# Second attention, its queries and its output projection in one stage; first attention's query products moved to its head; shorter expert chain

## The reference

```python
x = x + _L0_xattn_ref(_layernorm(x), ctx_1024, ctx_1024, mask, Wq, bq, Wk, bk, Wv, bv)   # first attention
x = x + _L0_attn_ref(_layernorm(x), ...)      # time mixing with a scan, channel mixing
x = x + _L0_ffn_ref(_layernorm(x), ...)       # 8 experts, the best 2
x = x + _L1_xattn_ref(_layernorm(x), ctx_1024, wq, wk, wv, wo, ln_gamma, ln_beta)        # second attention
x = x + _L1_attn_ref(_layernorm(x), ...)      # state-space scan
x = x + _L1_ffn_ref(_layernorm(x), ...)       # 8 experts, all added
```

```python
def bit_linear(x, w):
    xn = _rms_norm(x)
    xq = _ste(xn, _act_quant(xn))
    wq = _ste(w, _weight_quant(w))
    return jnp.einsum('bni,oi->bno', xq, wq)
q = bit_linear(x, wq); k = bit_linear(y, wk); v = bit_linear(y, wv)     # y: the context
out = softmax(q k / 4) v
out = layernorm(out) * ln_gamma + ln_beta
return bit_linear(out, wo)
```

## Time and profile before

| | |
|---|---|
| median of 3 runs | 1953.05 us (1948.78 to 1953.59) |
| profiled execution | 1950.69 us, span 1948.9 us |
| busy share of the span | PE 71%, DVE 69%, ACT 48%, POOL 39% |
| mean granted clock of TensorE | 0.826 of full speed |
| 38 to 206 us | first attention's tile loop |
| 682 to 758 | query stage and filling of the second attention |
| 758 to 1005 | second attention's loop over 64 batches |
| 1005 to 1058 | output projection |
| 1791 to 1949 | experts after the last scan |

### The profile page before, as it was taken

One profiled execution on the slowest core, in us unless ns is written; L12 is line 12 of the kernel. 1 busy time (PEld: TensorE's weight loads), 2 busy tenths in 40 slices (PEclk: granted clock), 3 DMA queues, 4 the chain that ended last, 5 costly groups with the idle time before them and its releaser, 6 DMA issues. The chain is left out here.

```text
span 1948.9 us, 33347 instructions
## 1 busy us (share of the span) xinstructions
PE 1383.8 (71%) x12585; PEld 772.4 (40%) x12585; DVE 1347.2 (69%) x2388; ACT 938.3 (48%) x1745; POOL 761.9 (39%) x808
## 2 busy tenths in 40 slices
PE   5889536988389514888842973445499788789998
PEld 4444223656254202555531421001145344345666
DVE  4548799961747683777769535998998899796110
ACT  2546333433134232555542434333398689676454
POOL 2325100000523123433410002664687788678433
PEclk9779777999669856999985985556599899899999
DMA  6557200000525235666621346798565465442000
GB/s 238 210 190 282 103 0 1 1 1 1 216 88 187 89 76 111 93 96 97 93 39 45 104 113 166 178 227 197 143 152 127 101 154 138 97 106 68 1 11 12
DMA packets 152100, 211.84 MB, mean 109 GB/s; under 512 B 107039, under 2 KB 112095, under 8 KB 138880
## 3 DMA queue, kind: packets, MB, share of 16 engines
q1 hardware_dynamic: 151940, 209.70, 41.5%
HBM read 154.85 MB, written 31.75 MB: 96 GB/s over the span
## 5 line engine op out<-in xcount | busy, mean ns | idle before, releaser
L2641 POOL TENSOR_TENSOR mf_st<-mf_st,mf_c_rep 128x1024 f32<-128x1024 f32 x128 | 300.9, 2351 | 339.0 <-DVE mf_st L2715 338.9
L2715 DVE TENSOR_TENSOR_SCAN mf_st<-mf_dA,mf_u_ps 128x512 f32<-128x512 f32 x256 | 310.3, 1212 | 0.0
L2543 PE MATMUL mf_y_ps<-mf_st,c_consts 128*32 128x512 f32 x512 | 155.9, 799 | 174.0 <-POOL mf_st L2641 127.1
L2826 ACT ACTIVATE mf_dA<-c_dt,c_neg_a 128x496 f32<-128x496 f32 x256 | 167.1, 701 | 108.6 <-DVE mf_st L2715 108.1
L2585 PE MATMUL mf_eh<-mf_parts,mf_w 128*128 128x512 f16 x768 | 197.4, 396 | 18.7 <-POOL mf_parts L2664 11.1
L2605 PE MATMUL mf_ey<-mf_w,mf_hid 128*128 128x256 f16 x1536 | 192.2, 276 | 0.0
L2709 DVE TENSOR_TENSOR mf_u_ps<-mf_st,mf_b_ps 128x512 f32<-128x512 f32 x256 | 177.7, 695 | 18.6 <-DMA mf_st<-xs 6.8
L2668 POOL TENSOR_TENSOR mf_hid<-mf_g,mf_hid 128x512 f16<-128x512 f32 x128 | 148.7, 1162 | 98.7 <-ACT mf_g L2843 98.6
L2605 PEld LDWEIGHTS mf_ey<-mf_w,mf_hid 128*128 128x128 f16 x1536 | 152.1, 99 | 49.3 <-issue 5.5
L2840 ACT ACTIVATE mf_hid<-mf_eh,c_vecs 128x512 f16<-128x512 f32 x128 | 88.0, 688 | 112.8 <-PE mf_eh L2585 112.3
L1978 ACT ACTIVATE t_p<-t_s_ps,t_mx 128x257 f32<-128x257 f32 x256 | 107.0, 474 | 46.8 <-DVE t_mx L2002 46.8
(11 more groups left out here) (485 smaller groups left out, 2834.3 us busy)
## 6 DMA issues: line engine op xcount, KB each, us to landing
mf_st<-xs SPq DMA_DIRECT2D x64, 1024.0 KB, 7.1
a_ctx_t<-in_ctx_t SPq DMA_DIRECT2D x16, 1024.0 KB, 7.2
a_ctx_n<-in_ctx_n SPq DMA_DIRECT2D x16, 1024.0 KB, 7.1
cqs<-a_whole_rows SPq DMA_DIRECT2D x16, 512.0 KB, 4.6
c_cq<-cqs SPq DMA_DIRECT2D x16, 512.0 KB, 13.4
mo_raw<-in_l_w SPq DMA_DIRECT2D x16, 512.0 KB, 3.7
ws<-mo_split SPq DMA_DIRECT2D x32, 256.0 KB, 2.3
mf_w<-ws SPq DMA_DIRECT2D x32, 256.0 KB, 8.6
```

The lines of the kernel that those rows point to most:

```text
L2543: m = e.matmul(y_ps[T * j:T * j + T, :], c.pick[:, gg, :], st[u % RING][:, j, :], start=(gg == 0), stop=(gg == 3))
L2641: e.tensor_tensor(half(u, h), half(u, h), over(c_rep[u // UNITS % 2][:, :], [P, 2, BT], 1), ALU.mult).then_inc(hcs("done"), 1)
L2715: e.tensor_tensor_scan(st[u % RING][:, j, :], dA[:, n % AHEAD, :], u_ps[j % 2][:, :], 0.0, ALU.mult, ALU.add).then_inc(hs("done"), 1)
L2826: e.activation(by_batch(dA[:, n % AHEAD, :])[:, :, 1:], dt, ACT.Exp, scale=c.neg_a[:, at:at + 1]).then_inc(dAs("done"), 1)
```

## The change

The query products of blocks 1 to 3 of the first attention leave the tile loop and stand in its head, through the banks `o_ps` and `y_ps`; the loop's `keep_busy` is three junk matmuls in every tile. The stages `l1_queries` and `l1_project` go; their work is placed by batch number in the streams of `l1_attention`: the queries of block 0 in its head, block i+1 from batch 16 i on, the projection of block i from batch 16 i + 25 on, the last one behind the loop. The integer context is loaded by SP in a ring of four buffers. The clears go to the start of `l1_prepare`. In `l1_blocks` DELAY is 5, and the positions are closer together.

```diff
@@ PE, head of the first attention @@
+            for i in range(1, BLOCKS):
+                for half in range(CJ):
+                    q_row(i, half)
+                q_constant(i)
             over_tiles(e, turns)
@@ second attention, where a set's pieces stand @@
+        def query(b, lag):
+            i, at = divmod(b - lag, BB)
+            return i + 1 if at == 0 and 0 <= i < BLOCKS - 1 else 0
+        def project_out(b, lag):
+            i, at = divmod(b - lag - BB - 9, BB)
+            return i if at == 0 and 0 <= i < BLOCKS - 1 else -1
+        def extras(b):
+            return ([("q", query(b, 7 + h), h) for h in range(2) if query(b, 7 + h) > 0] +
+                    [("x", project_out(b, 7 + h), h) for h in range(2) if project_out(b, 7 + h) >= 0])
@@ SP, in the loop over b @@
+                if b % BPT == 0 and b // BPT + 4 < GROUPS:
+                    load(b // BPT + 4)
+                if query(b, 5):
+                    turn_queries(query(b, 5))
+                for x in range(2):
+                    if query(b, 10 + x):
+                        send(query(b, 10 + x), x)
+                if project_out(b, 5) >= 0:
+                    turn_attended(project_out(b, 5))
@@ PE @@
                 if b + 1 < B:
                     score(b + 1, 0)
+                for tile in extras(b):
+                    rows(turn_of[tile], min(b + LEAD, B) - 1)
                 turn(b, 1)
@@ ACT, behind the exponentials of b+1 @@
+                if query(b, 1):
+                    row_std(e, q_var, q_std, qr, query(b, 1), c)
+                if query(b, 3):
+                    query_rt(query(b, 3))
+                if query(b, 9):
+                    round_query(query(b, 9))
+                if project_out(b, 1) >= 0:
+                    row_std(e, x_var, x_std, xr, project_out(b, 1), c)
+                if project_out(b, 3) >= 0:
+                    attended_rt(project_out(b, 3))
@@ DVE, at the end of a batch @@
+                if query(b, 0):
+                    moments(e, own, q_var, qr, q_tiles(query(b, 0)))
+                if query(b, 2):
+                    query_norm(query(b, 2))
+                if query(b, 4):
+                    query_ints(query(b, 4))
+                if project_out(b, 0) >= 0:
+                    attended_stats(project_out(b, 0))
+                if project_out(b, 2) >= 0:
+                    attended_norm(project_out(b, 2))
+                if project_out(b, 4) >= 0:
+                    attended_ints(project_out(b, 4))
@@ l1_prepare, SP @@
+            clear_spent(e, spent)
...
-FIRST, DELAY = UNITS + 2, 7
+FIRST, DELAY = UNITS + 2, 5
@@ l1_blocks, DVE @@
-                    if p == 1 and j == 0:
+                    if p == 0 and j == 3:
                         residual(b)
-                    if p == 1 and j == 3:
+                    if p == 1 and j == 1:
                         normalised(my, my_std, my_normed, b, r)
...
-            ring += [("turn", 2 * b + k) for k in range(2) if p == 5]
-            ring += [("logits", b)] if p == 6 else []
+            ring += [("turn", 2 * b + k) for k in range(2) if p == 3]
+            ring += [("logits", b)] if p == 4 else []
```

More of the change, by code:

```diff
@@ L676, in _ @@
             mask(0, 0)
+            keep_constant(1)
+            largest(0, 0)
+            for i in range(2, BLOCKS):
+                keep_constant(i)
             weight(0, 0)
-            largest(0, 0)
             rescale(0, 0)
@@ L744, in _ @@
                 features(i)
+            for i in range(1, BLOCKS):
+                keep_row(i)
             exponentials(0, 0)
@@ L1897, in _, with rows, project @@
                 end(b)
+                if query(b, 9):
+                    low_query(query(b, 9))
         @block.tensor
         def _(e):
-            def project(b):
+            def rows(n, b):
+                kind, i, h = ring[n]
+                r, turned, weight = (qr, q_turned, c.wq) if kind == "q" else (xr, x_turned, c.wo)
+                e.wait_ge(turned, (i + 1) * 16)
+                e.wait_ge(*drained.at("done", n - 1))
+                e.wait_ge(*keys.at("done", b))
+                e.wait_ge(*values.at("done", b))
+                for k in (2 * h, 2 * h + 1):
+                    for j in range(CJ):
+                        m = e.matmul(kv_ps[:, (k % 2) * C:(k % 2 + 1) * C], r.xT[:, k, j, :], weight[:, j, :],
+                                     start=(j == 0), stop=(j == CJ - 1))
+                m.then_inc(rows_t("done"), 1)
+            def project(b, n):
                 e.wait_ge(x_in[b // BPT % 2], (b // (2 * BPT) + 1) * 16)
@@ L1949, in out @@
                 i.then_inc(outs("done"), 1)
-            for s in (kv, *scores, *turned, outs):
+            for s in (kv, *scores, *turned, outs, rows_t):
                 s.start(e)
@@ L1969, in _ @@
                     turn(b + 1, 0)
+            for n in range(len(ring) - 4, len(ring)):
+                rows(n, B - 1)
         @block.scalar
@@ L2040, in combine, with query_norm, query_ints @@
                                 over(inv[u][:, :], [P, BPT * 4, HD], 2), ALU.mult).then_inc(whole("divided"), 1)
-            for s in (*maxes, kept[0], keys, values, whole):
+            def query_norm(i):
+                e.wait_ge(*q_squares.at("done", i - 1))
+                normalise(e, own, q_std, q_normed, qr, q_tiles(i), i)
+            def query_ints(i):
+                e.wait_ge(*q_normed.at("done", i))
+                if i:
+                    e.wait_ge(q_turned, i * 16)
+                quantise(e, own, q_rt, q_ints, qr, c.wf[:, 0:1], i)
@@ new lines, in attended_stats, with attended_norm @@
+            def attended_stats(i):
+                e.wait_ge(placed[i], BB * 16)
+                moments(e, own, x_var, xr, x_tiles(i))
+            def attended_norm(i):
+                r = xr
+                e.wait_ge(*x_squares.at("done", i - 1))
+                for k in range(KT_):
+                    e.scalar_tensor_tensor(r.big[:, k, :], x_tiles(i)[:, k, :], r.mean[:, k:k + 1], c.row["x_gamma"],
+                                           ALU.subtract, ALU.mult).then_inc(*own())
+                e.wait_ge(*own.now())
+                e.wait_ge(*x_std.at("done", i))
+                e.reciprocal(r.rstd[:, :], r.std[:, :]).then_inc(*own())
+                e.wait_ge(*own.now())
+                for k in range(KT_):
+                    e.scalar_tensor_tensor(r.xn[:, k, :], r.big[:, k, :], r.rstd[:, k:k + 1], c.row["x_beta"],
+                                           ALU.mult, ALU.add).then_inc(x_normed("done"), 1)
@@ L2043, in _ @@
+            for s in (*maxes, kept[0], keys, values, whole, q_var, q_normed, q_ints, x_var, x_normed, x_ints, drained):
                 s.start(e)
+            moments(e, own, q_var, qr, q_tiles(0))
+            query_norm(0)
+            query_ints(0)
             for b in range(LEAD):
@@ L2052, in _ @@
                     maximum(b + 1, 0)
+                for tile in extras(b):
+                    drain(turn_of[tile])
                 if b % BPT == 0 and b:
@@ L2157, in l1_inner @@
+            combine(GROUPS - 1)
+            for n in range(len(ring) - 4, len(ring) - 2):
+                drain(n)
+            attended_stats(BLOCKS - 1)
+            attended_norm(BLOCKS - 1)
+            attended_ints(BLOCKS - 1)
+            for n in range(len(ring) - 2, len(ring)):
+                drain(n)
 def l1_inner(nc, c):
@@ new lines, in build, with sb3 @@
+        if 3 in stages:
+            with ExitStack() as three:
+                def sb3(name, shape, dt=FP32):
+                    return three.enter_context(nc.sbuf_tensor(f"c_{name}", shape, dt))
+                c.parts = [sb3(f"parts{x}", [P, CJ, B * T], FP16) for x in range(2)]
+                c.we = [sb3(f"we{x}", [P, CJ, E * C], FP16) for x in range(2)]
+                c.gate, c.gate_t = sb3("gate", [P, TILES, E]), sb3("gate_t", [E, B * T])
+                l0_gates(nc, c)
+                l0_experts(nc, c)
```

460 lines of the change are left out of this document (167 added, 293 removed).

## The result

The changed kernel takes 1944.32 us, median of 20 runs (1932.0 to 1953.52), against 1952.8 of the kernel before in the same 20 rounds (1941.39 to 1960.53): ratio 0.9953, 95% interval 0.9933 to 0.9973. The profiled execution took 1932.22 us (span 1930.4) and is thus one of the fastest; its stages show where time went, but their sum is 12 us better than the median.

What follows compares the result with a forecast made beforehand. The second attention's loop was taken as bound by a chain through DVE, ACT and PE, its outer stages by engines taking turns. 1950.7 - 21 + 7 - 4 = 1933, with 2.4 for the median 1936 us; range 1908 to 1960.

Steps and rivals of the forecast that it cites:

- First attention: Query products moved from three long tiles to the head: 40.5 us out, 23 back, 3.7 in an existing wait; gain 21.
- Clears: Semaphore clears on SP moved ahead of the prepare stage's weight loads lose their cover: +5 us.
- Head and end: Second attention: first score comes 46 us sooner (40 to 50); the tail after the loop shrinks by 29 (25 to 33).
- Loop: Second attention's loop takes in three query and three projection sets: +77 us, bounds +9 and +116.
- my second rival: Second attention's loop slower than its pieces through clock and GpSimd; nothing gained from +94; at +105, 1964 us; chance 0.15.
- slack of 0.85 us: Second attention's loop: mean batch 3.86 us against a fast one of 3.01; slack used up in every batch of a set.
- four loads of a set: ACT table loads in the second attention's loop, as root and exponential alternate: 4 x 1.28 = 5.1 us per set.
- 116 us of pieces: Upper bound for the second attention's loop, nothing absorbed: 3 x 38.5 us for three query and three projection sets.
- Queue of SP: Added transfers in the second attention's loop delay no batch; if one did, 3.86 us per set; not in the sum.
- Expert chain: DELAY 7 to 5: 7 of 10.4 us gained at the end, some lost in the scan phase; net -4 (-10 to +5).
- Pieces hidden in idle time: Rival: added pieces vanish in DVE's and ACT's idle loop time; 1884 us, or 1910 with half hidden; chance 0.12.
- A drain behind each load: Rival: each table switch in the loop also drains ACT, +31 to +33 us, total 1967; chance 0.02.

Runs made afterwards that it cites:

- early: Changed kernel with all query blocks' statistics and deviations in the head, query root mean square made linear, clears behind the prepare stage's loads: 1929.62 us, 0.9865 of the kernel before.
- att_only: Kernel before with the second attention's part of the change alone (queries and projection in its loop, context ring, clears moved): 1.0165 of the kernel before, +32 us.
- no_loads: Changed kernel with the second attention's square roots replaced by a linear function, so no table loads in its loop: 0.9823 of the kernel before, loop 322.1 us.
- busy: Changed kernel with junk matmuls on PE in every batch that carries or follows a DVE or ACT piece: 1949.63 us, 0.9967 of the kernel before.
- q_only: Changed kernel with the output projection back in its own stage, queries still in the loop: 1934.78 us, 0.9897 of the kernel before, loop 302.9 us.
- pair: Changed kernel with query sets begun at batches 0, 12 and 24, so one runs beside a projection set: 1933.0 us, 0.987 of the kernel before.
- delay7: Kernel before with the expert chain's new positions alone, DELAY kept at 7: 0.9944 of the kernel before.
- blocks_only: Kernel before with the shorter expert chain alone (new positions and DELAY 5): 0.9936 of the kernel before, -12.5 us.

## Why the prediction came out as it did

Forecast 1936, faster; measured 1944.3, faster by 8.5 of the 17 us forecast. Direction and range are right, but partly by luck: the second attention cost 32 us where the sum had 7, and 9 us more from the first attention and 8 more from the expert chain, neither of them foreseen, made up for 17 of these 25.

**First attention: 21 us forecast, 30 measured alone (34 in the profile).** The head's products took 20.4 us, the lower bound of 21, not 23, and the first tile starts 14.4 us later, not 19. The larger miss was in the tiles: I took 7.8 us, the tile right behind a long one, for the usual tile. The kernel before already shows another: from 159.56 us on there is no long tile any more, and the six that follow take (202.63 - 159.56)/6 = 7.18 us each, at a clock of 1.00 (0.82 between 56 and 130 us):

```profile
202.63 0.38 ACT L703 ACTIVATE a_pt<-a_pt_ps 128x256 f32<-128x256 f32 x1 [1.71 <-PE a_pt_ps L512]
```

The tiles next to the long ones took 7.5 to 8.3. So a long tile cost more than itself: from the first to the last of the 16 tile starts on ACT it was 202.6 - 47.9 = 154.7 us and is 168.9 - 62.3 = 106.6, 48 less instead of 40.5.

**Clears: +5 forecast.** The prepare stage ends 24.3 instead of 19.2 us behind the experts, and early took the 5 us back. Right.

**Head and end: 46 and 29 us forecast.** Prepare's end to first scores went from 758.10 - 680.5 = 77.6 to 682.24 - 646.8 = 35.4: 42. The last transfer of the query's halves alone was waited for 7.48 us by PE, where I had 4 in the sum. From the last combine to the last drain 22.6 us, forecast 23. Right, the first by 4 us less.

**Loop: +77 forecast, +99.6 in the profile, 96 in att_only (726.7 to 1062.7).** This is the term that failed, by 20 us, and my second rival (from +94 on nothing is gained) was what happened to the loop; the kernel was saved by the other two parts. By the keeps of the changed kernel, against mean batches of before (3.81), the 30 batches with statistics, deviation, norm, root or integers are 73 us longer, the 12 with drains or rounding alone 17, and the 21 that hold no piece 10, of which 3.7 are one batch with a wait for SP's queue (below). So the sets' own batches took 90 where I had 77, and I had nothing for the batches between them.

Inside the sets' batches two errors work against each other. I had the slack of 0.85 us used up in each of them, 39 us in all. It was not: a projection's norm of 3.5 us makes a batch of 7.34 and its integers of 3.9 us one of 7.28, both 3.5 above the mean, where I had said 1 to 3; a query's norm of 1.5 us makes 4.42, 0.6 above it. And the four loads of a set cost not 5.1 but about 3 us (17 us for 24 in no_loads). My 116 us of pieces, with 17 for the loads instead of 31, are 102, so that some 12 us were absorbed and not 39; that is a sum, not a test. The clock, which I counted at nothing, is shown to fall to 0.78; its price is not shown separately, since no_loads and busy bound it only together with other work, and it stays open how much of the rest it makes.

**Queue of SP.** I wrote that no batch waits for it, since the keys are turned four batches ahead. One does plainly in the changed kernel: a transfer of context holds the queue 3.61 us, the keys' turn behind it is issued at 756.98 and PE starts the scores 3.42 us late:

```profile
752.63 3.61 SPq L1729 DMA_TRANSPOSE t_xT<-t_cq  x1
...
756.98 1.90 SPq L1738 DMA_TRANSPOSE t_kT<-t_parts  x1
...
760.06 0.60 PE L1885 MATMUL t_s_ps<-t_kT,c_qT 32*32 32x258 f16 x16 [3.42 <-issue]
```

A query's second send (3.19 us at 748.23) stands just ahead of it, as in q_only. In the kernel before the turnings of context took 2.5 us in the median, now 3.6. The price is that one batch (3.7 us above the mean) in the changed kernel, 11 us in q_only, where no integers of a projection cover the other two, and it appears in early and pair when other pieces are taken away or moved. I had named the right price, one batch's 3.86 per set, and given it no place in the sum. No run takes the transfers out of the queue.

**Expert chain: -4 forecast, -12.5 measured.** 5.3 came behind the scans where I let 7, and -4.9 in the scan phase where I had +3: the earlier residual does wait longer for PE (49.0 us in its eight instructions, 42.7 before), so something else in the new positions saves more; that it is norm and affine, now closer together, is my reading and not shown. The 10.3 us behind the scans that I cut to 7 came whole with DELAY alone (delay7 against blocks_only); the positions took 5 of them back there.

**Rivals.** Pieces hidden in idle time: no, DVE and ACT idle 101 and 152 us in the new loop. A drain behind each load, as the Trainium skill has it (ScalarE: Activation LUTs, What ACT_TABLE_LOAD costs): the root's load ends at 707.59 and the root starts at 707.60, the next activation at 707.81; no drain is seen, and 24 loads left out saved less than their own 31 us.

## What to carry to other kernels

An idle share of an engine inside a tight loop over several engines is not room: the longest pieces put between two steps of the chain (3.5 and 3.9 us) were paid to 3.5 us each, the batches without pieces grew too, and PE's clock fell (0.97 to 0.78). The projection's own stage at 53 us for four blocks (13 each) was cheaper than what its pieces added to the loop (36) plus the end that stays (23). Count the queue of transfers as one more engine on the chain: what is put into it ahead of the keys' turn delays PE. Where pieces must go in, put those of different engines into the same iteration, since they run side by side there; take out of the loop what needs another activation table; and measure the groups of a large change apart, as here two good parts covered a bad one of 32 us.

## What was not expected of the hardware

A table load whose turn comes while its engine would wait anyway costs next to nothing: of two roots a set, the deviation's two loads cost 0.5 and 0.9 us in the mean of the projection and the query sets, the other's two 2.9 in both (batches with and without loads compared). Nine junk matmuls a tile (2.4 us of PE at full clock) made no difference in time that can be told: 0.9846 with them, 0.9838 without, at clocks of 0.98 and 0.74. The stages of gates and experts, with unchanged code, take 156.8 or 161.5 us from one profiled execution to another; nothing here shows why.
